# First chunk of the attention loop prepared inside the stage of keys and values

## What is computed

```python
q = (layernorm(x) @ Wq + bq).reshape(H=16, 896, 16) / 4      # 16 heads of 16 columns
k, v = split(ctx @ Wkv + bkv)                                # 24,000 keys per head
q = round(q / sq) * sq        # sq = max|q| / 127 over the 16 columns
k = round(k / sk) * sk        # sk = max|k| / 127 over the 16 columns
v = round(v / sv) * sv        # sv = max|v| / 127 over ALL keys, per column
attn = softmax(q @ k.T)                                      # 896 x 24,000 per head
attn = round(attn / sa) * sa  # sa = max(attn) / 255 over the keys
x = x + (attn @ v) @ Wp + bp
```

## Time and profile before

| what | us |
|---|---|
| median of 3 runs | 5044.6 (5043.4 to 5048.5) |
| the profiled execution | 5051.2 |
| its span, first to last instruction | 5048.4 |
| span up to the last projections of keys and values | about 729 |
| engines start on attention | 780.9 |
| attention's first sums over keys | 816.5 |
| attention's last first-sweep maximum | 4294 |

### The profile page before, as it was taken

The page is one execution under the profiler, slowest core; times in us unless marked ns, Lnnn a source line. Parts: engine busy times, 40 slices in busy tenths (PEclk is TensorE's granted clock), DMA queues, the critical chain, the costliest instruction groups (busy, mean ns, idle before and its releaser), DMA issues. The chain is left out here.

```text
span 5048.4 us, 167274 instructions
## 1 busy us (share of the span) xinstructions
PE 4781.4 (95%) x53753; PEld 2024.0 (40%) x53753; DVE 4100.5 (81%) x7046; ACT 3919.3 (78%) x6649; POOL 3678.5 (73%) x3915
## 2 busy tenths in 40 slices
PE   4999987999999999999999999999999999887979
PEld 3666652333333333333333333333333333324645
DVE  4888887989889898989898988989898989673242
ACT  0555556999999999999999999999999999881110
POOL 1777775888888888888888888888888888761000
PEclk7999997999999999999999999999999999998989
DMA  2555542111111111111111111111111111432000
GB/s 64 149 156 162 161 136 55 32 33 30 33 33 30 30 35 32 31 32 31 32 33 31 32 31 33 32 32 32 31 32 34 31 32 46 143 113 84 35 1 8
DMA packets 222962, 270.06 MB, mean 53 GB/s; under 512 B 34299, under 2 KB 202899, under 8 KB 221379
## 3 DMA queue, kind: packets, MB, share of 16 engines
q1 hardware_dynamic: 168771, 205.60, 14.7%
q10 hardware_dynamic: 53376, 53.76, 3.3%
HBM read 174.76 MB, written 82.97 MB: 51 GB/s over the span
## 5 line engine op out<-in xcount | busy, mean ns | idle before, releaser
L1316 ACT ACTIVATE e<-ps_sweep,sk 125x448 f32<-125x448 f32 x6144 | 3505.2, 634 | 225.3 <-ACTq L1315 119.0
L1349 DVE TENSOR_REDUCE unit_max<-ps_sweep 128x1 f32<-128x500 f32 x5040 | 3036.7, 671 | 267.4 <-DVEq L1348 254.0
L1578 POOL TENSOR_SCALAR r<-e 125x896 f32<-125x896 f32 x2976 | 2788.3, 953 | 584.2 <-POOLq L1577 525.6
L1047 PE MATMUL ps_sweep<-q,k 54*128 54x448 bf16 x5760 | 1864.8, 354 | 7.8 <-PEq L1037 1.7
L1102 PE MATMUL ps_av<-e,zt 126*17 126x224 f32 x24576 | 1708.2, 353 | 0.0
L1078 PE MATMUL ps_sweep<-k,q 48*128 48x500 bf16 x5040 | 1556.9, 378 | 25.4 <-PEq L1077 21.8
L1097 PE MATMUL ps_av<-r,vt 125*16 125x224 f16 x12288 | 851.9, 267 | 29.0 <-PEq L1088 16.0
L1078 PEld LDWEIGHTS ps_sweep<-k,q 48*128 48x128 bf16 x5040 | 317.5, 94 | 1068.3 <-issue 1063.4
L1047 PEld LDWEIGHTS ps_sweep<-q,k 54*128 54x128 bf16 x5760 | 530.8, 93 | 518.9 <-issue 405.4
L1102 PEld LDWEIGHTS ps_av<-e,zt 126*17 126x17 f32 x24576 | 627.2, 96 | 0.6
L1097 PEld LDWEIGHTS ps_av<-r,vt 125*16 125x16 f16 x12288 | 300.3, 85 | 720.1 <-issue 719.9
(11 more groups left out here) (239 smaller groups left out, 3028.4 us busy)
## 6 DMA issues: line engine op xcount, KB each, us to landing
k_rows<-krows ACTq DMA_DIRECT2D x48, 1000.0 KB, 6.6
k<-k_rows SPq DMA_DIRECT2D x408, 93.8 KB
k<-k_rows SPq DMA_DIRECT2D x120, 281.2 KB
cx<-in_ctxT SPq DMA_DIRECT2D x48, 500.0 KB, 4.5
v_raw<-vb SPq DMA_DIRECT2D x24, 1000.0 KB
vr<-v_raw SPq DMA_DIRECT2D x128, 187.5 KB
cb<-in_ctxT SPq DMA_DIRECT2D x16, 1500.0 KB, 6.2
gu_w<-in_gu SPq DMA_DIRECT2D x5, 1536.0 KB, 10.8
```

What stands on the lines that cost most here:

```text
L1047: pe.matmul(score_bank(i, g, False)[:, 0:HALF], k2[u][:, i * KT:i * KT + P], q2[y][:, g * HALF:(g + 1) * HALF], start=True, stop=True, til ...
L1316: act.activation(e[i % SLOTS][0:KT, g, :], score_bank(i, g, both)[0:KT, 0:HALF], ACT.Exp, scale=sk[u][:, i:i + 1]).then_inc(e_wrote, 1)
L1349: top = dve.tensor_reduce(unit_max[:, b, j * NPIECE + at:j * NPIECE + at + 1], ps[:, 0:SB], axis=AX.X, op=ALU.max)
L1578: pool.tensor_scalar(r[i % SLOTS][:, :, :], e[i % SLOTS][0:KT, :, :], 1.0, HALFWORD, ALU.mult, ALU.add)\
```

## The change

The two stages stay, with their barrier. Several steps change place.

- The tiles of the first chunk, their semaphores and the helpers that load and prepare it are created outside both stages. SP issues the first chunk's loads in `keys_and_values`, in its turn for generation 31 (`STORED` is 30), after ACT has said by `chunk_stored` that the rows are stored. With it goes the second chunk's load for the maxima.
- DVE: the last `value_top` and `value_seen` stand behind the first seven of the last 28 maxima instead of ahead of all; `value_scales` stands ahead of the last seven; head 0's shift and its copies into `q2` follow the last maximum, ahead of the barrier.
- PE: the last generation's seven pieces are interleaved with `turn_scales`, and `shift_rows` follows them.
- POOL: the last `low_part` stands ahead of the last `scale_parts`; the reduction of `v_amax`, and scaling and rounding of the first chunk's values (now into `vt0`), follow. `less` and the pads of `k1`, `k2` are set at the stage's start.
- ACT: the last `mid_part` comes after two row copies; the Sigmoid of `decay` and a one-element Exp come ahead of the barrier.
- At the start of attention: no 9 early pieces for head 1, so its 336 pieces are spread over its 180 steps; the pads of `e` are set by DVE instead of POOL, with a semaphore for each slot; `zeros`, `zt`, `one` and `head_sel` stay on POOL.

```diff
+STORED = 30
@@ load_first_chunk, called by SP
+    def load_first_chunk():
+        load_first(1, 0, 0)
+        load_queries(1, 1)
+        load_values(0, 0)
+        load_second(0, 0, 0)
+        load_scaled_queries(0, 0)
+        load_first(1, 1, 1)
@@ keys_and_values, SP
+            sp.dma_start(decay[:, :], bcast(t["L1_xattn_decay"], P)).then_inc(decay_landed, 16)
+            sp.dma_start(sq[:, :, :], q_scale.rearrange("(b p) h -> p b h", p=QB)).then_inc(sq_landed, 16)
...
+                if n == STORED + 1:
+                    sp.wait_ge(chunk_stored, 1).then_inc(chunk_stored, -1)
+                    load_first_chunk()
@@ keys_and_values, PE
-            for n in range(NGEN + 4):
+            for n in range(NGEN + 3):
                 piece = pieces(n - 4)
                 for p in range(2):
                     project(n, p, piece)
                     turn(n - 3, 2 * p, piece)
-                if in_stage(n - 3) and batch_of(n - 3) is not None:
+                if in_stage(n - 3) and batch_of(n - 3) is not None and n - 3 < NGEN - 1:
                     turn_scales(batch_of(n - 3))
+            pe.wait_ge(scales_ready, 1).then_inc(scales_ready, -1)
+            piece = pieces(NGEN - 1)
+            turn_scales(NBATCH - 1, piece)
+            piece(NQB - 1)
+            shift_rows()
@@ keys_and_values, DVE
-            for half in range(2):
-                value_top(NGEN - 1, half)
-                value_seen(NGEN - 1, half)
             for n in range(NGEN - 4, NGEN):
                 for b in range(NQB):
                     maximum(n, b)
+                if n == NGEN - 4:
+                    for half in range(2):
+                        value_top(NGEN - 1, half)
+                        value_seen(NGEN - 1, half)
+                    dve.sem_inc(v_amax_ready, 1)
+                elif n == NGEN - 2:
+                    value_scales()
+            dve.wait_ge(sq_landed, 16).then_inc(sq_landed, -16)
+            head_max(0)
+            high_part()
+            other_parts()
+            for i, (lo, hi) in enumerate(((0, BANK), (BANK, TOK))):
+                dve.wait_ge(shift_turned, 1).then_inc(shift_turned, -1)
+                dve_done(dve.tensor_copy(q2[0][0:SROWS, lo:hi], ps1[i][0:SROWS, 0:hi - lo]))
+                dve.sem_inc(s_free, 1)
@@ keys_and_values, POOL
-                scale_parts(n)
+                if n < NGEN - 1:
+                    scale_parts(n)
             low_part(NGEN - 1)
+            scale_parts(NGEN - 1)
+            pool.sem_inc(scales_ready, 1)
+            pool.wait_ge(v_amax_ready, 1).then_inc(v_amax_ready, -1)
+            pool.partition_all_reduce(v_all[:, :], v_amax[:, :], KT, bass.bass_isa.ReduceOp.absmax)\
+                .then_inc(v_all_ready, 1)
+            pool.wait_ge(v_inv_ready, 1).then_inc(v_inv_ready, -1)
+            for half in range(2):
+                scaled_values(0, half)
+                whole_values(vt0, half)
@@ keys_and_values, ACT
+                if n - 2 == NGEN - 1:
+                    mid_part(n - 2)
...
+                if n == STORED:
+                    act.sem_inc(chunk_stored, 1)
+            act.wait_ge(decay_landed, 16).then_inc(decay_landed, -16)
+            act.activation(decay[:, :], decay[:, :], ACT.Sigmoid)
+            act.activation(warm[:, :], ident[0:1, 0:1], ACT.Exp)
@@ attention, PE
-            pe.wait_ge(less_ready, 1).then_inc(less_ready, -1)
-            for n in range(sum(EARLY)):
-                piece(n, 1)
-            shift_rows((0,))
-            pe.wait_ge(pads_ready, 1).then_inc(pads_ready, -1)
@@ attention, pieces of a step, on PE and DVE
-                        todo = pieces(j * CT + i, second, more)
+                        todo = pieces(j * CT + i, finished is not None, more)
@@ attention, DVE
-            dve.wait_ge(sq_landed, 16).then_inc(sq_landed, -16)
-            head_max(0)
-            high_part()
-            other_parts()
-            for n in range(sum(EARLY)):
-                piece(n, 1)
-            shift_rows(0, False)
-            value_scales()
+            for i in range(SLOTS):
+                dve_done(dve.memset(e[i][3 * QUAD:, :, :], OFFSET))
+                dve.sem_inc(pads_ready, 1)
@@ attention, POOL
-            for i in range(SLOTS):
-                pool_done(pool.memset(e[i][3 * QUAD:, :, :], OFFSET))
-            pool.sem_inc(pads_ready, 1)
-            pool.partition_all_reduce(v_all[:, :], v_amax[:, :], KT, bass.bass_isa.ReduceOp.absmax)\
-                .then_inc(v_all_ready, 1)
...
-            pool.wait_ge(v_inv_ready, 1).then_inc(v_inv_ready, -1)
-            for half in range(2):
-                scaled_values(0, half)
-                whole_values(0, half)
```

273 lines of the change are left out of this document (144 added, 129 removed).

## The result

| | before | after |
|---|---|---|
| median | 5046.2 (8 runs, 5040.5 to 5048.9) | 5034.2 (8 runs, 5031.2 to 5036.6) |
| ratio after / before | | 0.9977 [0.9966, 0.9988] |
| span of the profiled execution | 5048.4 | 5032.4 |

The kernel is 12.0 us faster (by the interval 6 to 17 us). The forecast was 5026.3 us with a range up to 5034.0, so the sign was right and the gain was forecast too large: 18.3 us. Two later comparisons gave 0.9975 [0.9966, 0.9984] and 0.9976 [0.9967, 0.9985], with medians of 5030.6 and 5031.0.

A forecast was written before the change was run, and what follows sets the result against it. The attention loop was taken as bound by PE and ACT, the winnable time as single waits between about 729 and 822 us. Terms -20.7 + 1.9 + 0.5 = -18.3 us took 5044.6 to 5026.3, range 5019 to 5034.

The forecast's parts named there:

- step 6: Restart behind the barrier to the loop's step 6: DVE's pads and folds 8.4 us; 15.9 instead of 36.6, 20.7 us less.
- step 7: First attention pass: nine more pieces fit DVE's idle share and cost PE at most 3.4 us; taken as 0.5 us.
- Step 5: Barrier between the stages: three ends within 1.4 us, restart 1.4 us behind the last, at 782.8, 1.9 us later than before.
- Step 1: Last 28 maxima: value maxima behind seven score maxima make everything behind, up to the last rows, 2.6 us early.
- Step 2: Stage's end, scores and scales interleaved: DVE's last maximum at 774.8 against 778.71, scales landing at most 0.7 us later.
- Step 3: Head 0's shift ahead of the barrier: 4.5 us from 774.8, then matmuls and copies 2.1 us, ending at 781.4.
- Step 4: First chunk's values ahead of the barrier: POOL's code loads and scaling end at 780.7; DVE's inverse costs nothing.
- Step 8: SP's loads in generation 31: eleven issues, 5.4 us of queue, cost nothing; up to 5.4 us if the cover failed.
- the rival of dear code loads: POOL's two code loads beside stores each take 3 us more; restart 5.3 us later, 5031.6 us; chance 0.12.
- The better start: Loop's start: the clock may rise early, worth 2.4 us, and DVE's pads be quicker, 4 us; 5022 us, chance 0.13.
- the start isn't set by what was moved: Dearer pads (1.5 us each, +4), nine pieces paid in full (+3), failed load cover (+5.4): 5038 us, no change, chance 0.04.
- The slower one: First pass: extra maxima tip DVE and PE waits for banks; decides from 0.10 us per step; 5062 us, chance 0.03.

The follow-up runs named there:

- tops_later: Kernel before with only the last generation's value maxima moved behind seven score maxima; ratio to the kernel before 0.9995 [0.9986, 1.0004].
- pads_direct: Changed kernel with DVE's eight pads signalled by the memset itself instead of waiting for each to complete; ratio to the kernel before 0.9968 [0.9956, 0.9980].
- nine_left_out: Changed kernel with head 1's nine early pieces made nowhere, so nine maxima are left out; ratio to the kernel before 0.9967 [0.9955, 0.9978].
- loads_behind: Changed kernel with the first chunk's key, query and scale loads behind the barrier again, values' load still ahead; ratio to the kernel before 0.9973 [0.9963, 0.9984].

## Why the prediction was right in sign and too large in size

The measured 5034.2 us lie outside the range. Two terms of the sum were too small: the eight pads on DVE in step 6 and the nine more pieces in step 7. What changes between the forecast and the traces, in its own steps:

| step | forecast | traces |
|---|---|---|
| 5, barrier (with 1 to 4) | 1.9 later | 1.1 later |
| 6, restart to step 6 | 20.7 earlier (15.9) | 17.8 earlier (18.5) |
| 7, nine more pieces | 0.5 | 2.2 |
| 8, loads in generation 31 | 0 | 0 |
| sum | -18.3 | -14.5 |

- **Step 1** held: tops_later moved the restart by 2.6 us. That it agrees to the tenth is luck: the step's own terms, 5.3 us less 2.4, give 2.9 and not the 2.6 that it states.
- **Step 2** held: the last maximum 4.4 us earlier (3.9 reckoned), the scales 0.4 later (at most 0.7). That the interleaving spends on the scales what step 1 had won was in the sum, as the barrier's 1.9 us.
- **Step 3** was 1.2 us too dear. The shift took 3.3 us, not 4.5, since most of its small operations take 0.17 or 0.18 us here; in the earlier trace rows they stood beside POOL's memsets (0.46 for the last copy). Two of them are longer in the rows above: the copy at 776.00 takes 0.34, and the subtraction at 774.71 takes 0.49 and ends at 775.20, where POOL's scaling that ran beside it ends at 775.17. The Trainium skill, SBUF — State Buffer, section "Who interferes with whom", says that a DVE instruction with two SBUF inputs contends with a GpSimd instruction that reads SBUF, over ports that the two share as an exclusive lock. By that rule DVE waits for POOL's end, and these two ends agree; but the subtraction at 775.67 has two inputs as well and took 0.18 us inside POOL's rounding of 775.39 to 776.30, which the rule does not account for.
- **Step 4** held in kind: load 6.26 us as in the earlier trace rows, the second 7.6 instead of 8.6, values whole at 45.1 us behind the mark and ahead of the shift. In the other traces with the first load ahead of the barrier it took up to 7.55 us and moved the restart by up to 1.1 us, so the rival of dear code loads was right in kind for its first load, at less than half of its 3 us; for the second load nothing speaks.
- **Step 5** came out 0.8 us cheaper, mostly by the shift of step 3: the last end stands at 778.96 and the restart 1.1 us behind it, not 1.4.
- **Step 6 failed in one term.** "Eight pads at 0.84 + 0.15 us (POOL's row; DVE has no such row, and I take the same)": the memset was right (0.81), the idle around its completion was not, 0.45 instead of 0.15 us. Eight pads at 1.25 instead of 0.99 us are 2.1 us, and the first maximum came 2.4 us later than reckoned (10.8 for 8.4). That this wait was the cost is shown by pads_direct, where it is gone and the first maximum comes 2.4 us earlier. The prediction had listed pads above 1.2 us as a sign that it would be wrong, and had a rival with 1.5. All else in the step came as written: PE's one long wait in step 2, 8.52 us, for DVE; none for the values, and the clock rose 4.2 us behind step 6 as against 4.6 before. A rise ahead of step 6, which the better start wanted, came in none of the sixteen traces.
- **Step 7 failed.** 2.2 us instead of 0.5 (2.4 by nine_left_out, which shows the cause). The argument was DVE's idle share and rows of the array that stand free. But PE was busy 268.3 of 270 us, and nine pieces cost two thirds of what their matmuls take (0.25 of 0.378 us). In the kernel before these nine stood in the start, where PE and DVE waited for something else and they were free; the step took them out of cover and priced them as if they kept it.
- **Step 8** held: from generation 28 to 47 the stage takes 256.4 us with the loads in generation 31, with the values' load alone (loads_behind), and in the kernel before. What the prediction did not see is that the loads are covered by the pads of step 6 too.

The two terms are 2.4 and 1.7 us, the cheaper barrier takes 0.8 back, and 0.5 us of step 6 stay, 0.3 of them because the second trace of the kernel before has 36.0 instead of 36.6. 14.5 us off the first median shown (5044.6) is 5030.1, inside the range; the median that was measured first, 5034.2, lies 4 us above that and 0.2 us above the range's end; 1.6 of the 4 us are the kernel before itself, which had 5046.2 beside it. The range had been drawn from bounds of terms in one trace and held nothing for executions that differ by several us outside the change.

Of the rivals, "the start isn't set by what was moved" named both terms that failed and overdrew them (pads at 1.5 us, measured 1.25; 3 us for the pieces, measured 2.2); its third, the loads of step 8, did not come. The measured median is nearer to its 5038 us than to the forecast's 5026.3. The slower one wanted 0.10 us per step, and 2.2 us over 186 steps are 0.012. The better start did not come, and of the dear loads only the part told under step 4.
